# Decoder layer on one Trainium2 core: weighted sums of the attention moved directly behind the bursts of scores

## The chip, the cores and the metric

One core of a Trainium2 chip. The engines are PE (TensorE; PEld is its loading of weights), DVE (VectorE), ACT (ScalarE) and POOL (GpSimd); all DMAs are issued by SP (SyncE) on one queue. The metric is the device time of one execution in microseconds, as the median of several runs.

## The reference

For 32 batches of 128 positions with 1024 features in float32: attention with 32 query heads and 8 key and value heads, then a convolution with three taps weighted by cosine similarities of a context, then a low-rank mixture, each added to its input and normalised. The change touches the attention alone:

```python
q = (hidden_states @ wq.T).reshape(b, s, N_HEADS, HEAD_DIM).transpose(0, 2, 1, 3)
k = (hidden_states @ wk.T).reshape(b, s, N_KV_HEADS, HEAD_DIM).transpose(0, 2, 1, 3)
v = (hidden_states @ wv.T).reshape(b, s, N_KV_HEADS, HEAD_DIM).transpose(0, 2, 1, 3)
q = q * cos[None, None] + _rotate_half(q) * sin[None, None]
k = k * cos[None, None] + _rotate_half(k) * sin[None, None]
...
scores = jnp.einsum('bhqd,bhkd->bhqk', q, k) / math.sqrt(HEAD_DIM)
...
attn = jax.nn.softmax(final, axis=-1)
out = jnp.einsum('bhqk,bhkd->bhqd', attn, v)
```

With 128 positions every key that is not in the future is allowed, so the mask is the causal one.

## The kernel before

The program has two parts with a barrier between them. Part 1 (`part1`, from line 144) computes projections, scores, softmax and weighted sums for the 32 batches and stores the sums in `ot_scratch`; part 2 (`part2`, line 886) does the output projection, the convolution, the mixture and the norms. Part 2 starts on every engine only when all engines have ended part 1.

Part 1 is a software pipeline written out by hand: each engine has a function `step(t, par)` that `steps` (line 86) calls for t = 0 to 33, most of them in a hardware loop. In step t PE projects batch t (keys and values, then two groups of queries, in 24 slots of three 128x512 matmuls: `project`, line 433), and works on the scores of batch a = t - 1 and the weighted sums of batch b = t - 2. A batch has two halves u = 0, 1 of its heads. Ahead of the projection of certain slots PE does:

- slots 1 and 13: `score` (line 463), a burst of 16 matmuls with 32 rows each, placed side by side in the array; four banks `s_ps` take them. A profile counts each float32 matmul of this kind twice;
- slot 9: `turn_q` of half 1 (transposes of queries, line 452); slot 22: that of half 0 of the next batch; slot 17: `turn_k` (transposes of keys, line 442);
- slot 9, behind the transposes: `weigh` (line 476) of half 0, four matmuls with 32 columns each; slot 17, ahead of `turn_k`: `weigh` of half 1. Both write the one bank `pv_ps`.

Around it: DVE rotates the projections (`rotate`, lines 545 to 553; for the keys it also copies the new values into `v_new`), then for each of eight groups p = 0 to 7 adds the mask and takes the minimum (`mask_min`, 563), inverts the sums (570) and transposes 32x32 blocks (`turn_p`, 578). ACT rounds x (`high_x`, 668), squares the context (676), copies turned queries and keys (`copy_q` 682, `copy_k` 687) from the one bank `turn_ps`, takes the exponentials (695) and reads `pv_ps` (`read_ot`, 706: half 0 at p = 3, half 1 at p = 6). POOL scales the probabilities (814) and adds the rotated parts. SP's `step` (line 371) issues in this order: the loads of x and of the context, `move_p(b, 1)`, which is ten DMAs from `blocks` to `pt` (line 306), the store of half 0 of `ot`, the store of the sums `csum`, `move_v(t)` (line 296: `v_new` to `v_t`), `move_p(a, 0)`, and the store of half 1. SP works in order, so each wait in this list holds what is behind it.

In the last steps (t = 31 to 33) the weights of part 2 are loaded and rounded, the output of the first two batches is loaded back and projected by PE in step 32, and ACT takes the root of the norms (`take_root`, 727) at the end of step 32.

Of the kernel before, what the change touches and what calls it, by code (L numbers as in the profile page):

```python
# [22 lines left out]
B, S, D = 32, 128, 1024  # L23
# [35 lines left out]
def after(t, per, k):  # L59

    return t * per + k
# [7 lines left out]
def wait(eng, sem, count):  # L69

    if isinstance(count, int) and count <= 0:
        return
    eng.wait_ge(sem, count)


def valid(t):

    return not isinstance(t, int) or 0 <= t < B
# [65 lines left out]
def part1(nc, ctx, weights, raw, halves, wo_ps, handoff, xT, ctx_in, wqkv, wo, wx, wb,  # L144
# [135 lines left out]
    @block.sync  # L280
    def _(sp):
        def load_x(t, par):
            wait(sp, x_lo, after(t - 2, 2, 2))
            sp.dma_start(xraw[:, par], xT[t]).then_inc(x_in[par], 16)

        def load_ctx(t):
            wait(sp, sq_done, after(t - 1, 1, 1))
            wait(sp, nb_done, after(t - 1, 2, 2))
            first = ctx_in[t, 0, 0:1]
            sp.dma_start(ctx_t[:], bass.AP(tensor=first.tensor, offset=first.offset,  # L290
                                           ap=[[CB * S, P], [1, (CB + 1) * S]])).then_inc(c_in, 16)

        def move_v(t, par):
            wait(sp, pv_done, after(t - 2, NU, NU))
            wait(sp, rope_read, after(t, NG, 1))
            sp.dma_start(v_t[:, par], v_new[:]).then_inc(v_in, 16)

        def move_p(a, u):

            if at_step(a, 0):  # L300
                sp.wait_ge(set_up, 2)
            wait(sp, turned, after(a, NC, NJ * (u + 1)))
            wait(sp, pv_done, after(a - 1, NU, u + 1))
            for qb in range(QB):
                for kb in range(qb + 1):
                    sp.dma_start(pt[kb * SB:(kb + 1) * SB, u, qb], blocks[qb * SB:(qb + 1) * SB, u, kb]
                                 ).then_inc(p_in[u], 16)

        def load_later(n):

            if n == 0:
                wait(sp, x_lo, 2 * B)
            elif n == 1:
                wait(sp, sq_done, B)
                wait(sp, nb_done, 2 * B)
            elif n == 2:
                wait(sp, sq_done, B)
            else:
                later_done(sp, max(m for m in range(n) if lands(m) == lands(n)))
            dst, arrived = landing[lands(n)], later_in[lands(n)]  # L320
            if n < KT:
                sp.dma_start(dst, wo[:, n, :]).then_inc(arrived, 16)
            elif n == KT + 1:
                sp.dma_start(dst, wb).then_inc(arrived, 16)
            else:
                sp.dma_start(dst[:, 0:TAPS * P], wx).then_inc(arrived, 16)

        def load_o(t):

            wait(sp, x_lo, 2 * (B - 1 + t))  # L330
            if t == 1:
                later_done(sp, KT - 2)
            for u in range(NU):
                wait(sp, ot_out[u], after(t, 16, 16))
            sp.dma_start(raw[:, t], ot_dram[t]).then_inc(o_in[t], 16)

        def load_sums():

            sums = cs_dram[0, 0, 0:1]
            sp.wait_ge(cs_out, 16 * B)  # L340
            sp.wait_ge(summed, B)
            for dst, at, width in ((sqs, 0, QD + 1), (nbs, D, QD)):
                sp.dma_start(dst, bass.AP(tensor=sums.tensor, offset=sums.offset + at,
                                          ap=[[2 * D, B], [QD, 4], [1, width]])).then_inc(cs_in, 16)

        def store_zeros():

            sp.wait_ge(set_up, 1)
            for row in range(2):
                sp.dma_start(sim_dram[:, row, 0:1], zero[0:B, :],  # L350
                             allow_slow_non_contiguous=True).then_inc(sim_out, 16)

        def store_own():

            sp.wait_ge(sim_made, 1)
            sp.dma_start(sim_row(sim_dram, 2, 0), own).then_inc(sim_out, 16)

        sp.dma_start(xraw[:, 0], xT[0]).then_inc(x_in[0], 16)
        for n in range(PIECES):
            wait(sp, w_lo, n - STAGES + 1)  # L360
            sp.dma_start(stage(n), wqkv[n // GP, :, (n % GP) * WK:(n % GP + 1) * WK, :]).then_inc(w_in[n % STAGES], 16)
            if n == GP + 1:
                sp.dma_start(rope_t[:], rope).then_inc(consts_in, 16)
                sp.dma_start(mask_t[:], mask).then_inc(consts_in, 16)
                sp.dma_start(id_t[:], ident).then_inc(consts_in, 16)
        load_x(1, 1)
        load_ctx(0)
        load_x(2, 0)
        store_zeros()

        def step(t, par):
            a, b = t - 1, t - 2
            if valid(t + 1):
                if not at_step(t, 0) and not at_step(t, 1):
                    load_x(t + 1, 1 - par)
                load_ctx(t + 1)
            if at_step(t, B - 1):
                load_later(0)
                load_later(1)
                load_o(0)  # L380
            if at_step(t, B):
                load_sums()
                load_later(5)
                load_later(6)
            if valid(b):
                move_p(b, 1)
                wait(sp, ot_read, after(b, NU, 1))
                sp.dma_start(ot_dram[b, :, 0:BANK], ot[:, 0]).then_inc(ot_out[0], 16)
            if at_step(t, LAST):
                store_own()  # L390
            if at_step(t, B):
                load_later(7)
                load_later(8)
                load_o(1)
                wait(sp, q_turned, NU * B)
                sp.dma_start(xn0[:], x[0]).then_inc(xn_in[0], 16)
            if valid(t):
                wait(sp, sq_done, after(t, 1, 1))
                wait(sp, summed, after(t, 1, 1))
                sums = cs_dram[t, 0, 0:1]  # L400
                sp.dma_start(bass.AP(tensor=sums.tensor, offset=sums.offset, ap=[[CB, P], [D, 2], [1, CB]]),
                             csum[:]).then_inc(cs_out, 16)
                move_v(t, par)
            if at_step(t, B - 1):
                load_later(2)
            if valid(a):
                move_p(a, 0)
            if at_step(t, B - 1):
                load_later(3)
            if at_step(t, B):  # L410
                load_later(9)
            if valid(b) and not at_step(b, B - 1):
                wait(sp, ot_read, after(b, NU, 2))
                sp.dma_start(ot_dram[b, :, BANK:D], ot[:, 1]).then_inc(ot_out[1], 16)
            if at_step(t, B - 1):
                load_later(4)

        steps(sp, step, 0, LAST, LEAD, TAIL)
        sp.wait_ge(ot_out[0], 16 * B)
        sp.wait_ge(ot_out[1], 16 * (B - 1))  # L420

    @block.tensor
    def _(pe):
# [70 lines left out]
                mm.then_inc(wo_done, 1)  # L494

        def step(t, par):
            a, b = t - 1, t - 2
            if at_step(t, 0):
                for s in range(SLOTS):
                    if s == 2 * KT:  # L500
# [7 lines left out]
            for s in range(SLOTS):  # L508
                if valid(a):
                    if s % (NJ * PERIOD) == 1:  # L510
                        score(a, 1 - par, s // (NJ * PERIOD))
                    if s == 9:
                        turn_q(a, 1)
                if valid(b):
                    if s == 9:
                        weigh(b, par, 0)
                    if s == 17:
                        weigh(b, par, 1)
                if valid(t):
                    if s == 17:  # L520
                        turn_k(t)
                    if s == 22:
                        turn_q(t, 0)
                    if not (at_step(t, 1) and s < AHEAD):
                        project(t, par, s // KT, s % KT)
                if at_step(t, B) and s % PERIOD > 0:
                    project_out(s % PERIOD - 1, s // PERIOD)
# [136 lines left out]
    def _(act):  # L664
# [68 lines left out]
            nc.scalar.copy(halves[:, t, 0].rearrange("p t s -> p (t s)"), raw[:, t]).then_inc(o_hi, 1)  # L733

        def step(t, par):
            a, b = t - 1, t - 2
            if at_step(t, 0):
                copy_k(0, 0)
                high_x(1, 1)
# [5 lines left out]
            for p in range(NC):  # L745
                if p == 3 and valid(a):
                    copy_q(a, 1)
                if p == 2 and valid(t + 1):
                    high_x(t + 1, 1 - par)
                if p == 3 and valid(b):  # L750
                    read_ot(b, 0)
                if p == 6 and valid(b):
                    read_ot(b, 1)
                if p == 6 and valid(t):
                    copy_k(t, par)
                if p == 7 and valid(t):
# [20 lines left out]
                        high_later(9)  # L777
            if at_step(t, B):
                take_root()

        steps(act, step, 0, LAST, LEAD, TAIL)

# [703 lines left out]
```

## Time and profile before

| | |
|---|---|
| Runs | 1433.77 us median of 3 (1432.33 to 1434.33) |
| Profiled execution | 1433.92 us, its span 1432.1 us |
| PE busy | 1366.3 us (95%), mean granted clock 0.981 |
| DVE, ACT, POOL busy | 1091.3, 931.8, 985.1 us (76%, 65%, 69%) |
| Part 1 | to about 780 us |

The span runs from the first to the last instruction of the profile, and the execution's own time is 1.8 us longer. Busy shares are averages over two parts with different limits. Of a line in the timeline the start is exact for matmuls, and its length is modelled: matmuls that follow each other overlap.

### The profile page before, as it was taken

How to read it: one execution, taken by the hardware profiler on the slowest of the kernel's cores; microseconds unless marked ns; L12 is line 12 of the kernel's file. 1: busy time of each engine (PE TensorE's matmuls, PEld its weight loads, DVE VectorE, ACT ScalarE, POOL GpSimd, SP SyncE). 2: the span in 40 equal slices, each digit the busy share in tenths (PEclk: the TensorE clock that was granted, in tenths of full speed). 3: DMA queues.
4: the chain of work that ended last, by engine and by line, in shares of the span. 5: the costliest groups of instructions: out<-in, count | busy, mean ns of one | idle time of the engine just before them, and what ended most of it. 6: DMA issues, size and time to landing. Idle time of an engine off the chain costs nothing. (4 is left out here: it accounts for less than half of the span.)

```text
span 1432.1 us, 32297 instructions
## 1 busy us (share of the span) xinstructions
PE 1366.3 (95%) x8288; PEld 1058.1 (74%) x8288; DVE 1091.3 (76%) x3869; ACT 931.8 (65%) x3258; POOL 985.1 (69%) x936
## 2 busy tenths in 40 slices
PE   6899999999999999999986799999999999999995
PEld 4677777777777777777753688888888888888873
DVE  5677777777777777777775487788887788887774
ACT  5787878788787887878874354555554555554543
POOL 3776777777777777777764666777776777776763
PEclk9999999999999999999996999999999999999997
DMA  7345445454454544545465866665666665656641
GB/s 242 105 124 152 148 119 152 118 153 135 128 152 120 156 125 135 153 118 154 123 189 173 203 151 166 176 151 158 163 157 163 176 153 157 165 154 162 160 118 45
DMA packets 108861, 213.03 MB, mean 149 GB/s; under 512 B 26640, under 2 KB 32272, under 8 KB 108816
## 3 DMA queue, kind: packets, MB, share of 16 engines
q1 hardware_dynamic: 108816, 212.51, 53.6%
q8 instruction: 18, 0.29, 0.1%
q14 instruction: 27, 0.22, 0.1%
HBM read 131.83 MB, written 34.47 MB: 116 GB/s over the span
## 5 line engine op out<-in xcount | busy, mean ns | idle before, releaser
L433 PE MATMUL wo_ps<-weights,halves 128*128 128x512 f32 x2304 | 572.2, 400 | 11.5 <-DVE weights L612 11.4
L433 PEld LDWEIGHTS wo_ps<-weights,halves 128*128 128x128 f32 x2304 | 422.8, 189 | 128.3 <-issue 34.3
L695 ACT ACTIVATE pexp<-sm,smin 128x128 f32<-128x128 f32 x1024 | 398.8, 393 | 123.5 <-DVE smin L563 121.6
L1043 PE MATMUL wo_ps<-weights,halves 128*128 128x512 f32 x1488 | 400.5, 402 | 2.0 <-DVE yz L1146 2.0
L814 POOL TENSOR_TENSOR pn<-pexp,prec 128x512 f32<-128x512 f32 x256 | 268.5, 1049 | 146.5 <-DVE prec L570 146.5
L1396 POOL TENSOR_TENSOR prods<-prod,prods 128x512 fp32r<-128x512 f32 x192 | 259.7, 1360 | 134.3 <-ACT prods L1290 129.2
L1043 PEld LDWEIGHTS wo_ps<-weights,halves 128*128 128x128 f32 x1488 | 273.0, 190 | 60.8 <-issue 3.7
L563 DVE CUSTOM_DVE_ANT_0 sm<-s_ps,mask_t 128x128 f32<-128x128 f32 x1024 | 231.9, 281 | 79.2 <-PE s_ps L463 79.0
L1290 ACT CAST prods<-prod 128x512 fp32r<-128x512 f32 x192 | 118.8, 621 | 165.7 <-DVE prod L1180 129.2
L1180 DVE TENSOR_TENSOR prod<-att,x 128x512 f32<-128x512 f32 x192 | 186.2, 985 | 13.7 <-DMA att<-sim_scratch 10.8
L695 ACT ACTIVATION_READ_ACCUMULATOR pexp<-sm,smin 128x1 f32 x1024 | 195.0, 190 | 0.0
L1054 PE MATMUL conv_ps<-prods,weights 128*128 128x512 f32 x576 | 168.0, 401 | 14.4 <-POOL prods L1396 14.4
L578 DVE STREAM_TRANSPOSE blocks<-pn 128x512 f32<-128x512 f32 x256 | 177.2, 692 | 1.6 <-POOL pn L814 1.5
L1054 PEld LDWEIGHTS conv_ps<-prods,weights 128*128 128x128 f32 x576 | 108.6, 190 | 43.1 <-POOL prods L1396 18.6
L1390 POOL TENSOR_TENSOR rstd<-var,power 128x1 f32<-128x1 f32 x96 | 76.7, 799 | 70.5 <-DVE var L1171 69.2
L1163 DVE BATCH_NORM_STATS2 stats<-yz 128x6 f32<-128x512 f32 x128 | 88.9, 695 | 4.4
L1384 POOL TENSOR_TENSOR halves<-raw,halves 128x512 fp32r<-128x512 f32 x60 | 90.4, 1508 | 2.0 <-ACT halves L1285 2.0
L463 PEld LDWEIGHTS s_ps<-kt,qt 32*128 32x128 f32 x2048 | 63.7, 188 | 31.1 <-issue 23.1
L570 DVE RECIPROCAL prec<-psum_row 128x4 f32<-128x4 f32 x256 | 44.9, 175 | 53.5 <-ACT pexp L695 53.1
L788 POOL TENSOR_TENSOR halves<-raw,halves 128x512 fp32r<-128x512 f32 x62 | 79.6, 1284 | 8.4 <-ACT halves L668 7.9
L563 DVE DVE_READ_ACCUMULATOR2_ANT smin<- 128x1 f32 x1024 | 84.9, 83 | 0.0
L795 POOL TENSOR_TENSOR nb<-ctx_t 128x512 f32<-128x512 f32 x64 | 82.5, 1290 | 1.6 <-DVE csum L591 1.6
(99 smaller groups left out, 1657.0 us busy)
## 6 DMA issues: line engine op xcount, KB each, us to landing
att<-sim_scratch SPq DMA_DIRECT2D x192, 252.0 KB
pt<-blocks SPq DMA_DIRECT2D x640, 64.0 KB, 2.0
ctx_t<-in_ctx SPq DMA_DIRECT2D x32, 576.0 KB, 4.4
raw<-in_xT SPq DMA_DIRECT2D x32, 512.0 KB, 3.7
raw<-ot_scratch SPq DMA_DIRECT2D x32, 512.0 KB, 6.5
xn<-in_x SPq DMA_DIRECT2D x32, 512.0 KB, 7.3
out<-late SPq DMA_DIRECT2D x32, 512.0 KB, 6.2
ot_scratch<-ot SPq DMA_DIRECT2D x63, 256.0 KB, 2.1
```

Source lines behind the costliest of these rows:

```text
L433: mm = pe.matmul(qkv_ps[(par + g) % 2][:], xs[:, par, xl, k], w_sb[:, wl, g, k], start=(k == 0 and n == 0), stop=(k == KT - 1 and n == 2))
L563: ins = dve.tensor_tensor_reduce(sm[:, c % 2, i * P:(i + 1) * P], s_ps[i][:, j * P:(j + 1) * P], mask_t[:], 1.0, 3e38, ALU.add, ALU.min, s ...
L578: dve.transpose(blocks[:, u, :, j], pn[:, c % 2].rearrange("p (i b k) -> p b i k", i=NI, b=QB)).then_inc(turned, 1)
L695: ins = nc.scalar.activation(pexp[:, c % 2, i * P:(i + 1) * P], sm[:, c % 2, i * P:(i + 1) * P], ACT.Exp, bias=smin[:, c % 2, i:i + 1], sc ...
L814: pool.tensor_tensor(pn[:, c % 2].rearrange("p (i s) -> p i s", i=NI), pexp[:, c % 2].rearrange("p (i s) -> p i s", i=NI), prec[:, c % 2]. ...
L1043: mm = pe.matmul(wo_ps[n][:], os_t[:, par, ol, k], wo_sb[:, wl, k, n * BANK:(n + 1) * BANK], start=(k == 0 and m == 0), stop=(k == KT - 1 ...
L1054: mm = pe.matmul(conv_ps[h][:], wx_sb[:, wl, k], prods[:, m % PB, xl], start=(k == 0 and n == 0), stop=(k == TAPS - 1 and n == 2))
L1163: dve.bn_stats(stats[n][:, half], src[:, half * BANK:(half + 1) * BANK]).then_inc(counted[n], 1)
L1180: dve.tensor_tensor(prod[:, m % PB], att[:, k, h * BANK:(h + 1) * BANK], x1[:, par, h * BANK + k:h * BANK + k + BANK], ALU.mult).then_inc( ...
L1290: nc.scalar.copy(prods[:, m % PB, 0], prod[:, m % PB]).then_inc(prod_hi, 1)
L1384: pool.tensor_tensor(lo, oraw[:, par, cols], hi.bitcast(F32), ALU.subtract).then_inc(o_lo, 1)
L1396: pool.tensor_tensor(prods[:, m % PB, 1], prod[:, m % PB], prods[:, m % PB, 0].bitcast(F32), ALU.subtract).then_inc(prod_lo, 1)
```

## The change

- PE: `weigh` of half 0 moves from slot 9 (behind the transposes of queries) to slot 13, directly behind the second burst of scores. `weigh` of half 1 moves from slot 17 to slot 1 of the following step, directly behind the first burst. In the last step (t = 33) half 1 of the last batch stays in slot 17.
- ACT: `read_ot` of half 0 moves from p = 3 to p = 5, that of half 1 from p = 6 to p = 1 of the following step; for the last batch it stands at the end of step 33.
- SP: `move_v(a)` is issued a step later, between the loads and `move_p(b, 1)`; the wait for the first weighted sum stands ahead of the store of `csum` instead of in `move_p(a, 0)`; the store of half 1 stands behind `move_p(b, 1)` a step later, and that of half 0 at the end of the step. In the last step the store of half 1 of batch 30 stands ahead of `move_p(31, 1)`.

```diff
 (SP, move_p)
-            wait(sp, pv_done, after(a - 1, NU, u + 1))
+            if u == 1:
+                wait(sp, pv_done, after(a - 1, NU, NU))
...
 (SP, step)
-            a, b = t - 1, t - 2
+            a, b, c = t - 1, t - 2, t - 3
+            if at_step(t, 1):
+                move_v(0, 0)
...
-            if valid(b):
+            if valid(a) and not at_step(t, 1):
+                move_v(a, 1 - par)
+            if valid(b) and not at_step(t, LAST):
                 move_p(b, 1)
-                wait(sp, ot_read, after(b, NU, 1))
-                sp.dma_start(ot_dram[b, :, 0:BANK], ot[:, 0]).then_inc(ot_out[0], 16)
+            if valid(c):
+                wait(sp, ot_read, after(c, NU, 2))
+                sp.dma_start(ot_dram[c, :, BANK:D], ot[:, 1]).then_inc(ot_out[1], 16)
+            if at_step(t, LAST):
+                move_p(b, 1)
             if at_step(t, LAST):
                 store_own()
...
+            if valid(a):
+                wait(sp, pv_done, after(a - 1, NU, 1))
             if valid(t):
                 wait(sp, sq_done, after(t, 1, 1))
                 wait(sp, summed, after(t, 1, 1))
...
-                move_v(t, par)
...
-            if valid(b) and not at_step(b, B - 1):
-                wait(sp, ot_read, after(b, NU, 2))
-                sp.dma_start(ot_dram[b, :, BANK:D], ot[:, 1]).then_inc(ot_out[1], 16)
+            if valid(b):
+                wait(sp, ot_read, after(b, NU, 1))
+                sp.dma_start(ot_dram[b, :, 0:BANK], ot[:, 0]).then_inc(ot_out[0], 16)
...
 (PE, step)
-                if valid(b):
-                    if s == 9:
-                        weigh(b, par, 0)
-                    if s == 17:
-                        weigh(b, par, 1)
+                if s == 1 and valid(c):
+                    weigh(c, 1 - par, 1)
+                if s == 1 + NJ * PERIOD and valid(b):
+                    weigh(b, par, 0)
+                if s == 17 and at_step(t, LAST):
+                    weigh(b, par, 1)
...
 (ACT, step)
-                if p == 3 and valid(b):
+                if p == 1 and valid(c):
+                    read_ot(c, 1)
+                if p == 5 and valid(b):
                     read_ot(b, 0)
-                if p == 6 and valid(b):
-                    read_ot(b, 1)
...
             if at_step(t, B):
                 take_root()
+            if at_step(t, LAST):
+                read_ot(b, 1)
```

In PE's program a full step reads so before, from its first burst of scores (`s_ps`) over the transposes of queries (`turn_ps<-id_t,xn`), the weighted sums (`pv_ps`) and the transposes of keys (`id_t,kx`):

```order
L463 MATMUL s_ps<-kt,qt 128x128 x16
L433 MATMUL wo_ps<-weights,halves 128x512 x24
L452 MATMUL turn_ps<-id_t,xn 128x128 x4
L476 MATMUL pv_ps<-pt,v_t 32x512 x4
L433 MATMUL wo_ps<-weights,halves 128x512 x12
L463 MATMUL s_ps<-kt,qt 128x128 x16
L433 MATMUL wo_ps<-weights,halves 128x512 x12
L476 MATMUL pv_ps<-pt,v_t 32x512 x4
L442 MATMUL turn_ps<-id_t,kx 128x128 x2
```

and so with the change (lines are nine further down, 472 is `score`, 485 `weigh`):

```order
L472 MATMUL s_ps<-kt,qt 128x128 x16
L485 MATMUL pv_ps<-pt,v_t 32x512 x4
L442 MATMUL wo_ps<-weights,halves 128x512 x24
L461 MATMUL turn_ps<-id_t,xn 128x128 x4
L442 MATMUL wo_ps<-weights,halves 128x512 x12
L472 MATMUL s_ps<-kt,qt 128x128 x16
L485 MATMUL pv_ps<-pt,v_t 32x512 x4
L442 MATMUL wo_ps<-weights,halves 128x512 x12
L451 MATMUL turn_ps<-id_t,kx 128x128 x2
```

Both weighted sums now stand behind bursts, the 24 and the two times 12 projections are as many as before, and each kind of transpose has projections on both sides.

At the end of part 1 SP issues before, from the load of `wb` on (`[waits ...]` names the semaphores that an instruction waits for; `ot_read` counts ACT's reads of `pv_ps`):

```order
L324 DMA ctx_t<-in_wb 128x1024 [waits later_lo_dve]
L414 DMA ot_scratch<-ot 128x512 [waits ot_read]
L306 DMA pt<-blocks 32x512 [waits pv_done,turned]
L306 DMA pt<-blocks 32x512 x9
L388 DMA ot_scratch<-ot 128x512 [waits ot_read]
L356 DMA sim_scratch<-raw 32x4x256 [waits sim_made]
L137 UNCONDITIONAL_BRANCH [waits ot_out1,ot_out0]
```

and with the change:

```order
L325 DMA ctx_t<-in_wb 128x1024 [waits later_lo_dve]
L423 DMA ot_scratch<-ot 128x512 [waits ot_read]
L394 DMA ot_scratch<-ot 128x512 [waits ot_read]
L307 DMA pt<-blocks 32x512 [waits pv_done,turned]
L307 DMA pt<-blocks 32x512 x9
L357 DMA sim_scratch<-raw 32x4x256 [waits sim_made]
L423 DMA ot_scratch<-ot 128x512 [waits ot_read]
L137 UNCONDITIONAL_BRANCH [waits ot_out1,ot_out0]
```

Ahead of the last ten moves now stand two stores. The second, L394, is that of half 1 of batch 30, which in the program before stood in step 32 as L414; it waits for a read that ACT does in step 33, behind `take_root`.

## Rows read from the trace of the kernel before

**Rows 1.** Busy time in a stretch: PE, PEld, DVE, ACT, POOL; clock, DMA share, GB/s.
```profile
82.50:712.60 630.10, 630.10 (x4537) 463.63 (x4536) 491.94 (x2465) 510.44 (x2409) 460.25 (x421) 1.00 0.46 138
```
**Rows 2.** Timeline of PE, part of a step: start, length, line, what, [idle before].
```profile
404.27 0.60 PE L452 MATMUL turn_ps<-id_t,xn 128*128 128x128 f32 x4
404.80 1.07 PE L476 MATMUL pv_ps<-pt,v_t 128*32 128x512 f32 x8
405.80 3.01 PE L433 MATMUL wo_ps<-weights,halves 128*128 128x512 f32 x12
408.74 0.98 PEld L463 LDWEIGHTS s_ps<-kt,qt 32*128 32x128 f32 x32 [0.35 <-issue]
408.74 1.17 PE L463 MATMUL s_ps<-kt,qt 32*128 32x128 f32 x32
409.85 3.01 PE L433 MATMUL wo_ps<-weights,halves 128*128 128x512 f32 x12
412.79 1.06 PE L476 MATMUL pv_ps<-pt,v_t 128*32 128x512 f32 x8
413.79 0.44 PE L442 MATMUL turn_ps<-id_t,kx 128*128 128x128 f32 x2
413.98 3.66 PE L433 MATMUL wo_ps<-weights,halves 128*128 128x512 f32 x15
417.48 0.60 PE L452 MATMUL turn_ps<-id_t,qn 128*128 128x128 f32 x4
417.84 2.33 PE L433 MATMUL wo_ps<-weights,halves 128*128 128x512 f32 x9
420.10 1.17 PE L463 MATMUL s_ps<-kt,qt 32*128 32x128 f32 x32
```
**Rows 3.** Timeline of DVE and ACT behind the second burst of that step.
```profile
412.22 0.69 DVE L545 TENSOR_TENSOR rot<-wo_ps,rope_t 128x512 f32<-128x512 f32 x1 [0.43 <-PE wo_ps L433]
...
415.94 0.56 ACT L706 COPY ot<-pv_ps 128x512 f32<-128x512 f32 x1
416.40 0.36 ACT L687 COPY kt<-turn_ps 128x256 f32<-128x256 f32 x1
```
**Rows 4.** Timeline of SP and ACT; last, the page's issues (KB, us to landing).
```profile
399.63 0.36 SPq L284 DMA_DIRECT2D raw<-in_xT  x1
...
402.68 6.21 SPq L306 DMA_DIRECT2D pt<-blocks  x10
...
415.06 6.21 SPq L306 DMA_DIRECT2D pt<-blocks  x10
...
404.39 1.05 ACT L668 CAST halves<-raw 128x1024 fp32r<-128x1024 f32 x1 [1.00 <-DMA raw<-in_xT]
...
406.89 0.56 ACT L682 COPY qt<-turn_ps 128x512 f32<-128x512 f32 x1
...
raw<-in_xT SPq DMA_DIRECT2D x32, 512.0 KB, 3.7
```
**Rows 5.** Timeline of SP and PE, steps 1 and 2.
```profile
56.50 1.45 SPq L296 DMA_DIRECT2D v_t<-v_new  x1
...
71.22 1.17 PE L463 MATMUL s_ps<-kt,qt 32*128 32x128 f32 x32 [1.36 <-ACT qt L682]
```
**Rows 6.** Timeline of PE, second burst of step 31.
```profile
724.68 1.17 PE L463 MATMUL s_ps<-kt,qt 32*128 32x128 f32 x32 [0.82 <-ACT qt L682]
```
**Rows 7.** Timeline of PE, SP and ACT at the end of part 1.
```profile
752.24 2.09 PE L463 MATMUL s_ps<-kt,qt 32*128 32x128 f32 x32 [3.00 <-ACT qt L682]
...
768.80 6.21 SPq L306 DMA_DIRECT2D pt<-blocks  x10
...
772.39 0.57 ACT L706 COPY ot<-pv_ps 128x512 f32<-128x512 f32 x1
...
776.45 1.94 PE L476 MATMUL pv_ps<-pt,v_t 128*32 128x512 f32 x8 [7.61 <-DMA pt<-blocks]
...
780.36 1.19 PE L1043 MATMUL wo_ps<-weights,halves 128*128 128x512 f32 x2 [1.97 <-DVE yz L1146]
```

More of the change, by code:

```diff
@@ L496, in step @@
         def step(t, par):
-            a, b = t - 1, t - 2
+            a, b, c = t - 1, t - 2, t - 3
             if at_step(t, 0):
@@ L735, in step @@
         def step(t, par):
-            a, b = t - 1, t - 2
+            a, b, c = t - 1, t - 2, t - 3
             if at_step(t, 0):
```

## The prediction

> **What bounds the kernel now.** I read the busy time by stretches first [rows 1]. Over 630.1 us, 28 steps of the attention half at 22.50 each, PE is busy for all 630.1 at the full granted clock, while DVE has 491.9, ACT 510.4 and POOL 460.3. PE sets the pace there, and what can be won is what PE spends when it goes from one shape of tile to another. The timeline of PE from one transpose of queries to the next first burst [rows 2] shows that. Starts are what counts in it; the length of a block overlaps with what follows. The reader is to see:
> - Twelve projections and the change to a weighted sum take 412.79 - 409.85 = 2.94, nine and the change to scores 420.10 - 417.84 = 2.26: three fewer for 0.68, 0.227 for one.
> - Fifteen before a transpose take 417.48 - 413.98 = 3.50; less three, 2.82. So leaving full-size matmuls for tiles of 32 costs 0.12 more than leaving them for a transpose.
> - Transpose to weighted sum takes 404.80 - 404.27 = 0.53, transpose to projection 417.84 - 417.48 = 0.36: 0.17 less.
> - Score burst to projection takes 409.85 - 408.74 = 1.11, weighted sum to projection 405.80 - 404.80 = 1.00, weighted sum to transpose 413.79 - 412.79 = 1.00. What a weighted sum costs does not depend on which of the two follows.
>
> **The change, part by part.** Durations are from the profiled execution, 1433.92 us around a span of 1432.1. That is 0.15 over the median of the three runs; the difference is put on the median, 1433.77. A measurement of this kernel can tell about 0.2%, 2.9 us, from no change.
>
> *PE, a full step.* The first weighted sum no longer follows a transpose, so that transpose goes into projections: -0.17. The second no longer ends twelve projections; they end in the transpose of the keys: -0.12. That transpose now stands behind a full matmul; 413.98 - 413.79 = 0.19 is what it takes behind a weighted sum, two transposes of the queries' kind take 0.36 / 2 = 0.18 or, less a change, under that, so I bound the gain by 0 and 0.05 and take 0.03. The change from scores to a weighted sum stands in no row. The nearest row leaves a burst at 1.11 for projections; I take that and no extra, and the rivals have the other end. Sum: -0.32 a step, to 22.18. Steps 3 to 30 are 28: -9.0.
>
> *What the weighted sums delay.* Both bursts now have 1.00 of weighted sum behind them, so the projection behind each ends 1.00 later against its burst. DVE's rotation at 412.22 waits for just that projection [rows 3]; so it, the masks behind it and the exponentials behind those move by 1.00. ACT's copy of the turned keys ends at 416.76. The read ahead of it, 415.94 to 416.40, is gone (-0.46), so it ends 0.54 later against the burst. PE's transpose at 417.48 needs it: 0.72 of slack, less 0.54, less the 0.15 that PE gains in this half, leaves 0.03. That is a tie, and hundredths may go.
> The ten moves of probabilities on SP start at 415.06 behind DVE, and now 1.00 later; the load of x stands behind them [rows 4]. Against the next first burst, itself 0.1 nearer, it is 1.1 later. From its issue at 399.63 to ACT's rounding at 404.39 it takes 4.8 here, and ACT waited 1.00 for it; the copy of the queries ends at 407.45, 1.29 before the second burst at 408.74. Less 1.1, and less the 0.2 that PE gains before that burst, nothing is left. But this is a slow load: the page's median is 3.7, which leaves about 1 us. For both ties together I give back 0.4 over the loop, so it is worth -8.6.
> Covered, at nothing: ACT's read of the previous second sum (about 0.57), now ahead of the second exponential, lies in the wait for x; without that cover it would move the copy of the queries by 0.57. SP's move of the new values (put at one move's 0.62) now stands between the loads and the ten moves at 402.68. These start 3.05 behind the load of x with one other load between, so over 2 us are free, and the values are needed by a rotation that starts only with the last projections before 404.27; without the cover the ten moves, and so nothing before the weighted sum 20 us later, would wait. SP now waits for the first weighted sum, over 2.1 behind the second burst, before it stores the sums of squares; the ten moves behind start 415.06 - 408.74 = 6.3 behind the burst, so the wait ends first.
>
> *Start.* In step 2 the second burst waits at 71.22, 1.36 of it idle, for a copy that is behind x [rows 5]. The move of the values at 56.50, 1.45 long, stands ahead of ten moves and that load. It goes behind the load, so the burst comes 1.45 earlier; PE is ready for it, as the weighted sum no longer stands ahead of it. With the second half of that step: -1.6.
>
> *Step 31.* The load of the first attention output is again issued behind the ten moves, so 1.1 later, and the second burst at 724.68 waits for what follows from it, 0.82 already [rows 6]. What comes after hangs on this burst: +1.1. A load of weights no longer stands behind SP's wait for the second weighted sum and may free some of what follows; the bounds are 0 and -1.1 (it cannot give more than the delay), and I take 0, since no row shows that it held anything.
>
> *The end of the attention half* [rows 7]. The last ten moves are issued at 768.80 and land for the weighted sum at 776.45; part 2 begins on PE at 780.36, behind it and a barrier. The changed SP first stores the second sum of batch 30, which ACT must have read, and ACT reads it only behind the square root, in the place where it reads the first sum of batch 31 now: 772.39. ACT has one read more ahead of the second burst at 752.24, which waits for ACT: +0.57, so 772.96, and the read ends at 773.5. Then 0.1, a store of 0.62, ten moves of 6.21, and the 1.44 from the moves' end (775.01) to the sum: 781.9 against 776.45, +5.4. Part 2 can start nothing before, so this is paid in full.
>
> **Sum:** -1.6 - 8.6 + 1.1 + 5.4 = -3.7, so **1430.1 us**. Over half of what the loop gains is given back at the end.
>
> A rule beside the trace: in the rows PE pays when it enters or leaves tiles of 32. The Trainium skill (TensorEngine Tiling (Array Packing), Key Properties) says that "Changing tiling mode (not just tile) drains the TensorE". By it the change from the row tiles of the scores to the column tiles of the weighted sum is one more drain, so a step goes from eight changes of mode to six; it gives no price. With the rows' 0.12 to 0.17 as the price of one, two fewer would be worth 0.24 to 0.34 a step, where my differences give 0.32.
>
> **Rivals.**
> *A, slower: scores to weighted sum is a dear change.* No row has it. The first weight load of a burst stands idle for 0.35 before 408.74 [rows 2]. If the column tiles wait that long for the row tiles on top of the 1.11, twice a step, the step gains 0.32 and loses 0.70: 28 x 0.38 = +10.6, with -1.6 + 1.1 + 5.4 = +4.9: 1449. With an extra of 0.12 each, as for leaving full matmuls, 0.08 a step is left: -2.2 + 4.9 makes 1436.5. It decides from 0.10 a change on, where the loop's 28 x 0.12 = 3.4 no longer pays for the 4.9. Against it: the weighted sum's own leaving is the same for two followers. Chance 0.13, half for each price.
> *B, the later load of x becomes the bound.* If it takes 4.8 and a little more in all steps, the second burst waits some 0.2 in each: 28 x 0.12 = -3.4 in place of -8.6, so 1435.3. For it: ACT waits for x in the step shown. Against: the median of 3.7. Chance 0.12.
> *C, the end costs nothing*, as something else holds part 2: -9.1, 1424.7. Against it: the 7.61 that PE stands idle for these very moves. Chance 0.08.
>
> **How the numbers follow.** The forecast has 0.67, and by itself lies between 1427.5 and 1432.5: the loop -7.0 (0.25 a step) to -9.9 (0.35), step 31 up to 1.1 lower, the end 4.5 to 6. The range is 1425.5 to 1435.5, which takes in B and part of C and leaves A out. Faster by over 0.2% means below 1430.9: C and 0.75 of the forecast, 0.58. Slower means above 1436.6: the dear half of A and some of the other half, 0.10. The rest, 0.32, lies within.
>
> **What would show it.** In the profile after: steps of 22.2 with PE busy throughout; the weighted sum 1.1 behind the start of a burst and 1.0 to the projections; hundredths of idle time for the copies of keys and queries; x rounded about 1 us later behind the first burst; the second burst of step 2 near 69.7; the last ten moves behind a read that follows the square root, the last two weighted sums both behind it and some 8 us apart, and part 2's first matmul near 776.6 (780.36 - 3.7). Steps above 22.3 would make the loop's term wrong, over 1.2 from burst to weighted sum would be A, a second burst that waits in each step B, and a first matmul of part 2 near 771 C.

## The result, and the profile after

The changed kernel takes **1447.84 us** (median of 4 runs, 1445.97 to 1451.50) against 1433.05 for the kernel before on the same chip (4 runs, 1431.35 to 1434.33): ratio 1.011, 95% interval 1.0091 to 1.0128. It is slower, by 15 us, where 3.7 faster was forecast. The profiled execution has a span of 1444.1 against 1432.1, so 12.0 us are there to be found. (This execution is 1.9 below the median of its kernel and the one before 0.9 above its own, which makes the rest.)

The busy time of PE in the 28 full steps, with the same columns as [rows 1], comes first:

```profile
85.50:717.20 631.70, 624.37 (x4537) 462.55 (x4536) 488.94 (x2465) 512.59 (x2410) 460.45 (x421) 1.00 0.47 137
```

PE's work in this stretch fell from 630.10 to 624.37, 0.20 a step: the changes between shapes of tile are cheaper, as forecast. But the stretch got longer, 631.7. PE now stands idle for 7.3 us in it, and did not before. The waits of the whole execution (engine, line, what it waited for: us in total, times, longest) name the cause:

```profile
DVE v_new L563 <- DMA v_t<-v_new: 50.3, 31, 4.4
...
PE s_ps L472 <- DVE smin L573: 15.9, 18, 4.3
```

Before, DVE's copy into `v_new` waited for the move of the values once, 0.7 us. Now it waits in every step but the first. One such step, SP, DVE and PE, in the timeline (start, length, line, what, [idle before]):

```profile
225.72 0.36 SPq L284 DMA_DIRECT2D raw<-in_xT  x1
226.34 0.35 SPq L290 DMA_DIRECT2D ctx_t<-in_ctx  x1
226.91 0.52 SPq L296 DMA_DIRECT2D v_t<-v_new  x1
```
```profile
230.55 0.41 DVE L560 TENSOR_TENSOR rot<-wo_ps,rope_t 128x256 f32<-128x256 f32 x1
233.46 0.42 DVE L563 COPY v_new<-wo_ps 128x256 f32<-128x256 f32 x1 [2.50 <-DMA v_t<-v_new]
```
```profile
234.78 1.17 PE L472 MATMUL s_ps<-kt,qt 32*128 32x128 f32 x32 [1.10 <-DVE smin L573]
```

The reader is to see one chain. `v_new` is a single buffer. The move out of it is issued at 226.91, right behind 1.1 MB of loads, and has not landed when the next values are ready at 230.96. DVE waits 2.50 with the minima of the next masks (`smin`) queued behind the copy, and the second burst needs the banks that these masks free: PE waits 1.10. It does so in 15 of the 28 steps. The row on how long the move takes from issue to landing, of the kernel before and of the changed one:

```profile
DMA to landing us min/median/max: 2.0/2.0/3.0
```
```profile
DMA to landing us min/median/max: 2.1/5.2/7.3
```

A step that this wait does not reach looks as forecast (ten of the 28 lie within 0.01 of it):

```profile
627.49 1.17 PE L472 MATMUL s_ps<-kt,qt 32*128 32x128 f32 x32
628.59 1.06 PE L485 MATMUL pv_ps<-pt,v_t 128*32 128x512 f32 x8
629.59 5.75 PE L442 MATMUL wo_ps<-weights,halves 128*128 128x512 f32 x24
635.18 0.60 PE L461 MATMUL turn_ps<-id_t,xn 128*128 128x128 f32 x4
635.54 3.02 PE L442 MATMUL wo_ps<-weights,halves 128*128 128x512 f32 x12
638.48 1.17 PE L472 MATMUL s_ps<-kt,qt 32*128 32x128 f32 x32
639.59 1.07 PE L485 MATMUL pv_ps<-pt,v_t 128*32 128x512 f32 x8
640.58 3.04 PE L442 MATMUL wo_ps<-weights,halves 128*128 128x512 f32 x12
643.45 0.38 PE L451 MATMUL turn_ps<-id_t,kx 128*128 128x128 f32 x2
643.59 3.70 PE L442 MATMUL wo_ps<-weights,halves 128*128 128x512 f32 x15
647.12 0.63 PE L461 MATMUL turn_ps<-id_t,qn 128*128 128x128 f32 x4
647.50 2.32 PE L442 MATMUL wo_ps<-weights,halves 128*128 128x512 f32 x9
649.75 1.17 PE L472 MATMUL s_ps<-kt,qt 32*128 32x128 f32 x32
```

It takes 649.75 - 627.49 = 22.26, where 22.18 was forecast. Burst to weighted sum is 1.10, weighted sum to projections 1.00. Rival A's dear change does not exist.

Step 2, which answers to [rows 5], and step 31, to [rows 6], on PE:

```profile
72.08 2.09 PE L472 MATMUL s_ps<-kt,qt 32*128 32x128 f32 x32 [4.32 <-DVE smin L573]
74.10 1.94 PE L485 MATMUL pv_ps<-pt,v_t 128*32 128x512 f32 x8
...
731.20 1.38 PE L472 MATMUL s_ps<-kt,qt 32*128 32x128 f32 x32 [2.93 <-DVE smin L573]
732.51 1.94 PE L485 MATMUL pv_ps<-pt,v_t 128*32 128x512 f32 x8
```

Both second bursts wait for the same masks. Behind the longer idle time the burst and the weighted sum of step 2 take 2.09 and 1.94 in place of 1.17 and 1.06: they run at 1.2 GHz, not 2.4. In step 31 they take 1.38 and 1.94, and the granted clock is 0.66 over 731 to 736. The windows around step 2 (the number before the last two is the granted clock) say so:

```profile
57.00:70.00 13.00, 10.62 (x75) 8.19 (x73) 7.69 (x40) 10.23 (x52) 10.13 (x9) 0.99 0.58 167
70.00:76.00 6.00, 3.92 (x41) 2.06 (x41) 4.67 (x22) 2.85 (x14) 3.45 (x4) 0.50 0.28 70
```

The end of part 1, which answers to [rows 7], on ACT, SP and PE:

```profile
777.50 1.04 ACT L725 CAST weights<-ctx_t 128x1024 fp32r<-128x1024 f32 x1 [3.84 <-DMA ctx_t<-in_wb]
...
780.18 0.57 ACT L716 COPY ot<-pv_ps 128x512 f32<-128x512 f32 x1
```
```profile
780.77 0.34 SPq L394 DMA_DIRECT2D ot_scratch<-ot  x1
781.21 6.22 SPq L307 DMA_DIRECT2D pt<-blocks  x10
```
```profile
780.89 1.93 PE L485 MATMUL pv_ps<-pt,v_t 128*32 128x512 f32 x8 [9.28 <-ACT ot L716]
788.87 1.94 PE L485 MATMUL pv_ps<-pt,v_t 128*32 128x512 f32 x8 [6.04 <-DMA pt<-blocks]
792.78 2.47 PE L1055 MATMUL wo_ps<-weights,halves 128*128 128x512 f32 x5 [1.98 <-DVE yz L1158]
```

This is the mechanism of the forecast: the read behind the square root, the store, the ten moves, and two weighted sums 8.0 apart.

The 12.0 us, cut at the starts of PE's first bursts of steps 2, 3, 31 and 32 and at part 2's first matmul, beside the experiments below (the stretches are from single profiled executions, in us; the last column but one is the ratio to the kernel before that was run beside each, and the last the median of its own runs; the kernel before had 1433.05 beside the changed kernel and 1431.75 to 1431.93 beside e1 to e10):

| kernel | step 2 | steps 3 to 30 | step 31 | step 32 to part 2 | ratio (95%) | median |
|---|---|---|---|---|---|---|
| before | 24.87 | 630.09 | 24.17 | 43.55 | | |
| changed | 27.76 | 631.73 | 27.09 | 48.48 | 1.0110 (1.0091 to 1.0128) | 1447.84 |
| e1 | 25.11 | 624.69 | 24.63 | 50.06 | 1.0016 (1.0004 to 1.0028) | 1434.71 |
| e2 | 25.95 | 624.98 | 24.82 | 48.60 | 1.0021 (1.0008 to 1.0033) | 1434.57 |
| e3 | 28.40 | 632.59 | 27.36 | 44.34 | 1.0077 (1.0060 to 1.0094) | 1444.39 |
| e4 | 27.76 | 632.49 | 24.59 | 42.99 | 1.0031 (1.0018 to 1.0044) | 1437.61 |
| e5 | 23.62 | 626.31 | 26.27 | 44.57 | 0.9988 (0.9979 to 0.9997) | 1429.71 |
| e6 | 27.33 | 627.95 | 29.12 | 42.48 | 1.0016 (1.0002 to 1.0031) | 1433.94 |
| e7 | 24.78 | 621.97 | 27.18 | 44.48 | 0.9958 (0.9945 to 0.9972) | 1426.40 |
| e8 | 25.18 | 623.58 | 27.18 | 50.40 | 1.0026 (1.0016 to 1.0036) | 1435.92 |
| e9 | 23.09 | 621.97 | 22.39 | 45.61 | 0.9932 (0.9916 to 0.9948) | 1422.56 |
| e10 | 24.53 | 630.09 | 23.29 | 43.67 | 0.9994 (0.9983 to 1.0004) | 1431.67 |

So +2.9, +1.6, +2.9 and +4.9 for the change; what lies ahead and part 2 make up the rest (-0.4).

### The profile page after: what moved, and what is told of

It reads as the page before. It is cut to its first block and busy times, and to the rows that moved or that the text cites. A ratio compares the mean times of both kernels' runs of the same rounds, so it can differ in the third digit from the quotient of the medians.

```text
span 1444.1 us, 32306 instructions
## 1 busy us (share of the span) xinstructions
PE 1362.7 (94%) x8288; PEld 1057.7 (73%) x8288; DVE 1089.8 (75%) x3869; ACT 934.6 (65%) x3258; POOL 983.4 (68%) x936
## 5 line engine op out<-in xcount | busy, mean ns | idle before, releaser
L472 PE MATMUL s_ps<-kt,qt 32*128 32x128 f32 x2048 | 77.1, 288 | 21.8 <-DVE smin L573 15.9
L821 POOL TENSOR_TENSOR qn<-rot 128x512 f32<-128x512 f32 x32 | 41.4, 1293 | 71.7 <-DVE rot L560 71.7
```

What stands on the lines that cost most here:

```text
L472: mm = pe.matmul(s_ps[i][:, j * P:(j + 1) * P], qt[rows, u, j * P:(j + 1) * P], kt[rows, par, u * P:(u + 1) * P], start=True, stop=True, t ...
```

## The experiments

The theory, called V: the single buffer `v_new`, held by a move that lands late behind the loads, costs the loop its gain and disturbs steps 2 and 31. Its rivals stand in each expectation by their letters (X is the later load of x, D a DVE that has become too full). For the end there is theory E: the store ahead of the last moves costs about 4.

**e1: a second buffer for the new values.**

```diff
-    v_new = sb("v_new", [P, KV])
+    v_new = sb("v_new", [P, 2, KV])
...
-            sp.dma_start(v_t[:, par], v_new[:]).then_inc(v_in, 16)
+            sp.dma_start(v_t[:, par], v_new[:, par]).then_inc(v_in, 16)
...
-                wait(dve, v_in, after(t, 16, 0))
-                ins = dve.tensor_copy(v_new[:], src[:, KV:2 * KV])
+                wait(dve, v_in, after(t - 1, 16, 0))
+                ins = dve.tensor_copy(v_new[:, par], src[:, KV:2 * KV])
```

> The changed kernel with two buffers for the new values, so that the copy into v_new no longer waits for the move of the batch before. Theory V (the late move of the values holds DVE, and through the masks the second burst): no wait of DVE for v_t<-v_new, all full steps at the 22.27 us that the undisturbed ones have now (28 x 0.29 = 8 us less), the start of step 2 about 4 us less, step 31 about 2 us less; 1433 to 1435 us. Theory X (the late load of x holds the second burst): steps stay at 22.5 to 22.6 and PE waits for ACT's copy of the queries; 1443 to 1447 us. Theory D (DVE as a whole has become too full, the wait for the values only fills a gap): likewise above 1442 us, with PE waiting for the masks.

The move still lands late, but DVE is gone from those who wait, and POOL, whose work follows the copy, waits at the two ends alone, as it did before:

```profile
who waited for it (us, times):
  POOL kx L814: 15.4, 2
...
DMA to landing us min/median/max: 2.4/5.3/7.1
```

The loop falls by 7.0 against the changed kernel, to 22.31 a step, and the time from 1.0110 to 1.0016 of the kernel before. V holds: the wait, not the transfer, was the cost. The rivals X and D fall, since the load of x and the work of DVE are as they were. At the end e1 gives 1.6 back. Of this, 0.9 lies ahead of the second burst of step 32, which waits for ACT's copy (16.45 behind the first burst, 15.52 in the changed kernel), and 0.7 in the last ten moves, which SP issues in 6.93 here and in 6.22 there; what lies behind either was not tried.

**e2: the same move, issued ahead of the two loads.**

```diff
+            if valid(a) and not at_step(t, 1):
+                move_v(a, 1 - par)
             if valid(t + 1):
...
-            if valid(a) and not at_step(t, 1):
-                move_v(a, 1 - par)
             if valid(b) and not at_step(t, LAST):
```

> The changed kernel with one buffer, but the move of the values issued ahead of the loads of x and of the context. Theory V with the queue as its cause (the 0.13 MB wait behind the 1.1 MB of both loads): landing back from 5.2 to about 2 to 2.5 us, no wait of DVE for the values, while x comes 0.6 us later and takes some of it back: steps of 22.3 to 22.45 us, 1435 to 1440 us. If the landing is late for another reason (the write itself, the wait for the weighted sum), it stays near 5 us and the time near 1447 us.

```profile
  DVE v_new L563: 0.5, 1
...
DMA to landing us min/median/max: 2.0/2.1/4.9
```

The single buffer is back, and the wait is gone all the same: with the loads behind it the move lands in 2.1, not 5.2. So it is the place behind the loads that makes it late. The time, 1434.57, is just below the range.

**e4: the kernel before, with the move of the values alone a step later**, in the place that the change gives it (between the loads and `move_p(b, 1)`).

```diff
+            if at_step(t, 1):
+                move_v(0, 0)
...
+            if valid(a) and not at_step(t, 1):
+                move_v(a, 1 - par)
             if valid(b):
                 move_p(b, 1)
...
-                move_v(t, par)
```

> The kernel before with nothing changed but the move of the values, issued a step later behind the loads of x and the context, as in the changed kernel. Theory V: landing near 5 us here too, DVE waits for it over 1 us a step, but in this order the projection of the keys ends 1 us earlier against the burst and the second burst is 0.2 us later, so that little of it reaches PE: 1433 to 1438 us. If the late move alone were the whole loss, 1446 us or more; if the landing is 2 us here, the queue is not what made it late.

```profile
DVE v_new L556 <- DMA v_t<-v_new: 49.2, 31, 3.9
```

The wait is as long as in the changed kernel, 49.2 against 50.3, with nothing else of the change in it, and the time is inside the range. Step 2 takes 27.76 as in the changed kernel. But the loop lost only 2.4. In the kernel before, DVE's copy into `v_new` starts 3.95 ahead of the second burst (median of steps 3 to 30); with the change and no wait, in e1, it starts 2.69 ahead, because the first weighted sum no longer stands between the keys' projection and that burst (e6, which moves that sum alone, has 2.78). Where the wait holds the burst, the copy starts 1.32 ahead of it. So the old order takes up 2.6 of waiting before PE feels it, and the new one 1.4. The median wait is 1.3 in e4 and 1.6 in the changed kernel: most waits fit into the old order's room, and 15 of 28 do not fit into the new one's. The part is worth +0.3% alone and 0.9% in the whole: costs of this kind do not add.

**e8: the changed kernel, with x loaded one load earlier**, so that only the context stands ahead of the move. The loop's load goes from the start of the step, `load_x(t + 1, 1 - par)`, to a place ahead of `move_p(a, 0)` in the step before, as `load_x(t + 2, par)`.

> The changed kernel with the load of x alone moved ahead of the ten moves one step earlier, so that only the load of the context (0.58 MB) is in front of the move of the values, not x (0.52 MB) as well. If the landing is late by what is queued ahead of it, it falls from 5.2 us to 3 to 4 us, DVE waits less than 0.8 us a step, PE's waits for the masks go in most steps: 1438 to 1442 us. If the landing does not fall, the loads ahead are not its cause, and the time stays at 1445 us or more.

```profile
DVE v_new L563 <- DMA v_t<-v_new: 7.7, 6, 4.4
...
DMA to landing us min/median/max: 2.7/3.8/7.5
```

It went further than expected, 1435.92 against 1438 to 1442. The move lands in 3.8 in the median (not 5.2), which is below the 4 that the copy leaves it. In step 31, where three half-megabyte loads stand ahead of the move, DVE still waits 4.45, and the step takes 27.18. Three ways to make the move early enough, or not needed, give the same time within 0.1%.

**e3: the last ten moves ahead of the store.** In the last step `move_p(b, 1)` stands where it stands in all others, ahead of the store of half 1 of batch 30.

> The changed kernel with, in step 33 alone, the last ten moves ahead of the store of the second sum of batch 30. Theory E (the end is late since these moves stand behind that store): the ten moves start near 775.8 instead of 781.2 in the time of the changed kernel, part 2 starts 5 us earlier, 1442 to 1443.5 us. If part 2 is held by something else (the read of the sums behind the square root), under 2 us are won, 1446 us or more.

```profile
783.62 1.94 PE L483 MATMUL pv_ps<-pt,v_t 128*32 128x512 f32 x8 [9.69 <-ACT ot L714]
786.34 1.94 PE L483 MATMUL pv_ps<-pt,v_t 128*32 128x512 f32 x8 [0.79 <-ACT ot L714]
791.12 9.17 PE L1053 MATMUL wo_ps<-weights,halves 128*128 128x512 f32 x31 [2.84 <-DVE yz L1156]
```

The two sums are 2.7 apart, not 8.0, and the stretch to part 2 falls from 48.48 to 44.34. The ten moves now start at 778.35, ahead of the read at 782.91. E is right about the stretch. The time, 1444.39, is between the two ranges given: steps 2 to 31 of this execution happen to take 1.8 more than in the changed kernel, and the two ratios, 1.0077 and 1.0110, have intervals that overlap by 0.0003. The gain in the whole time is clear only between e1 and e5. What is left is the read behind the square root; ahead of the root ACT waits 3.98 for the load of `wb` (3.84 in the changed kernel).

**e5: e1 and e3 together.**

> The changed kernel with both single repairs together: two buffers for the new values, and the last ten moves ahead of the store of the second sum of batch 30. If the late values and the late end are two separate costs, this lies 4 to 5 us below the two buffers alone: 1429 to 1431 us, where before has about 1432, with full steps of 22.3 us and 43.5 to 45 us from the first burst of step 32 to part 2. If the end only waits for the next thing (the root, the sums of the cosine), it stays above 1433 us.

1429.71, ratio 0.9988: inside, and 0.28% below e1. With its two costs repaired, the change is barely worth having.

**e6: the first weighted sum alone.** The kernel before, with three edits; the second half, and the move of the values, stay where they were.

```diff
-                    if s == 9:
+                    if s == 1 + NJ * PERIOD:
                         weigh(b, par, 0)
...
-                if p == 3 and valid(b):
+                if p == 5 and valid(b):
                     read_ot(b, 0)
```

And SP stores half 0 behind the move of the values, no longer behind `move_p(b, 1)`.

> The kernel before with the first weighted sum alone moved behind the second burst (read at p = 5, its store behind the move of the values); second half and values where they were. By the price of its change of tiles this is worth 0.17 us a step, 22.33 us, so 4.8 us in the loop, less about 1 us in step 31, and nothing is lost at the end: 1428 to 1429.5 us, a ratio of 0.997 to 0.998. If the later projection of the second group of queries costs PE a wait, steps stay at 22.4 to 22.5 us and the time at 1431 to 1433 us.

A miss: 1433.94, ratio 1.0016, above both ranges. Full steps take 22.34, 0.16 less, just as the 0.17 for the transpose that now goes into projections says. But two of them, 4 and 5, take 23.45 and 23.44: x is rounded 5.6 and 4.7 behind its issue there, and the second burst stands idle 1.0 for the copy that follows. So the loop gains 2.1 and not 4.5. And steps 2 and 31 lose 2.5 and 4.9 in the profiled execution (itself 2.7 above the median of its runs):

```profile
70.26 1.58 PE L464 MATMUL s_ps<-kt,qt 32*128 32x128 f32 x32 [3.36 <-ACT qt L683]
71.78 1.94 PE L477 MATMUL pv_ps<-pt,v_t 128*32 128x512 f32 x8
...
726.25 2.09 PE L464 MATMUL s_ps<-kt,qt 32*128 32x128 f32 x32 [4.07 <-ACT qt L683]
728.27 1.72 PE L477 MATMUL pv_ps<-pt,v_t 128*32 128x512 f32 x8
```

The weighted sum that stood ahead of this burst filled 1.2 us of a wait for x (in step 31, for the first output). In step 2 of the kernel before it also cut PE's idle time in two, 0.90 ahead of it and 1.36 ahead of the burst:

```profile
65.85 1.06 PE L476 MATMUL pv_ps<-pt,v_t 128*32 128x512 f32 x8 [0.90 <-DMA pt<-blocks]
```

Where a load holds the burst, taking work from ahead of it gains nothing and puts 1.0 behind it; the idle time grows, and with it comes the lower clock: 1.52 and 1.86 for burst and sum in step 2, 2.02 and 1.64 in step 31, in place of 1.1 and 1.0. For step 2 that is the whole 2.5: -0.1 ahead of the burst, 1.0 for the sum, 1.6 for the clock. In step 31 the output's load also took 8.4 from issue to rounding (716.23 to 724.66), 6.3 before (716.79 to 723.09). Three loads are issued one behind the other there, the output's last, over 1.05 in e6 (from 715.18) and over 2.27 before (from 714.52); by my estimate that is 1.2 of the 2.1, and the rest stays open. No value waits for its move in this kernel, so this is a cost of the moved sum itself.

**e7: everything repaired.** e5, x early as in e8, and the copy of the keys one group earlier (`copy_k` at p = 5, ahead of the exponentials it followed).

> Both repairs, and two more: the load of x goes ahead of the ten moves of the first half one step earlier, and the copy of the turned keys on ACT ahead of the exponentials of p = 5. If the 0.1 us that a step of 22.27 us has over my sum of 22.18 is the tie at the keys and the late x, steps fall to 22.15 to 22.2 us, step 2 no longer waits for x, and the time is 1422 to 1427 us. If the sum itself was 0.1 us too low, steps stay at 22.27 us and only the start gains, 1427 to 1430 us.

1426.40, inside the range. All 28 full steps are 22.21, with PE busy throughout. In e8, with x as early and the copy of the keys where it was, 25 of them are 22.27. So the tie at that copy is worth 0.06 a step; e7 differs from e8 in the buffers too, but e1, which has them, also shows 22.27. In step 2 ACT no longer waits for x, as expected, but the second burst still stands idle 1.94 for ACT's copy.

**e9: e7, with the first output loaded ahead of the later weights in step 31.** Step 31 had become the dearest place: a half-megabyte load stands third of three.

```diff
             if at_step(t, B - 1):
+                load_o(0)
                 load_later(0)
                 load_later(1)
-                load_o(0)
```

> The kernel of e7 with one thing more: in step 31 SP loads the first attention output ahead of the two loads of later weights, not behind them. In e7's trace that load is issued at 708.33, third of three loads of half a megabyte within 1.1 us, and the second burst of that step waits 3.23 us idle, after which the burst takes 2.09 and the weighted sum behind it 1.72 instead of 1.17 and 1.06. Theory Q (the load waits its turn on the queue, and the idle time costs the clock on top): the output lands some 3 us earlier, the burst waits under 1.5 us and runs at full clock, step 31 falls from 27.18 by 3 to 4 us; what it gains partly returns at the burst of step 32, which waits 4.21. Time 1423 to 1426. Rival R (its own transfer is the limit, wherever it stands): step 31 stays near 27 and the time near e7's, 1426 to 1427.

```profile
709.87 1.05 ACT L741 CAST halves<-raw 128x1024 fp32r<-128x1024 f32 x1 [0.31 <-DMA raw<-ot_scratch]
...
712.19 1.17 PE L470 MATMUL s_ps<-kt,qt 32*128 32x128 f32 x32
```

Issued at 705.67, the output is rounded at 709.87, 4.2 behind; in e7 it was issued at 708.33 and rounded at 715.54, 7.2 behind. Step 31 falls from 27.18 to 22.39, and the burst and the sum behind it run at full clock again. 1422.56, ratio 0.9932: slightly below the range, and faster than both kernels. It is faster than e7 too, though the intervals of the two ratios overlap by 0.0003; step 31 in the traces makes the case. (In the traces step 2 is also 1.7 shorter than in e7, which the exchange cannot have done; the last section comes back to it.)

**e10: the kernel before, with that exchange alone.**

> The kernel before with the same exchange of loads in step 31 alone. There the second burst of that step waits only 0.82, so there is little to win. Theory Q: step 31 falls from 24.17 by about 0.8, some of it given back in step 32: 1430.5 to 1432 against 1431.8 for the kernel before. Rival R: no change, 1431 to 1432.5. If it wins more than 1.5 us, step 31 was holding more than its burst.

1431.67, ratio 0.9994: no difference that can be told. Step 31 gains 0.88, as expected, and no more. The same repair is worth five times as much in the new order. There the burst stands idle 3.23, not 0.82, as the weighted sum no longer fills the wait and the output is rounded 7.2 behind its issue, not 6.3; and the lower clock behind it costs 1.6, where before the burst ran at full clock.

## Why the prediction was wrong, point by point

**The step that failed** is the one put as "Covered, at nothing" for SP's move of the new values. I counted what it costs SP to issue (0.62) and found over 2 us free; I looked for who reads the values, and not for who writes `v_new` next. DVE's copy is ready 4.0 behind the issue (230.96 - 226.91), and the move needed 2.0 to land in its old place. Behind the two loads it needs 5.2. No row of mine had its landing. The Trainium skill (DMA: Bandwidth & Descriptors, Queues, rings and completion order) says that descriptors are consumed in ring order on each DMA engine, and that the semaphore's increment "lands only after every earlier write from that SDMA engine". By it a small move behind 1.1 MB waits for them, and e2 agrees: 2.1 in front of them, 5.2 behind. Whether the small move waits for its turn or shares the DMA engines with the loads, no run here separates. The rule was in reach of the prediction and was not used. The step is worth 7.0 in the loop, 2.7 in step 2 and 2.5 in step 31 (e1 against the changed kernel), 0.94% by the ratios.

**The loop** was forecast at -8.6, and is +1.6; without the wait (e1) it is -5.4, and with both ties loosened (e7) -8.1. The terms of PE: the sum -0.32 stands at -0.29 there (22.50 - 22.21). Burst to weighted sum 1.11 assumed, 1.10 found. The transpose into projections, 0.36 forecast, 0.36 found (635.54 - 635.18). Twelve projections into a transpose 2.82 forecast, 2.87 found. The transpose of the keys gained 0.05 (0.14 against 0.19), the upper bound. Fifteen projections took 3.53 or 3.54, up to 0.04 over. The tie at the keys' copy (0.03 of slack) was called, and its 0.4 for both ties was too little: the keys' 0.06 a step is 1.7 over the loop, and x, at 22.31 - 22.27 in e1, 1.1 more.

**Step 2** was forecast at -1.6 and is +2.9. The earlier load did what was said: without the wait for the values (e1) the second burst comes 12.21 behind the first, not 13.54, 1.33 of the 1.45. What I missed stands behind it: 2.13 of idle time ahead of that burst, where 1.36 had been, and the clock at half. Burst and sum then take 1.6 more, which left e1 at +0.2. (In e1 PE waits there for the copy of the queries, not for the values.)

**Step 31** was forecast at +1.1. In e1 the burst comes 0.94 later, as said; the rest in the changed kernel, another 1.0 of wait for the values and the slow clock, was in no term.

**The end** was forecast at +5.4 and costs 4.9. The size is right and e3 shows the mechanism: it takes 4.1 of it back in this stretch, and 5.5 beside the two buffers (e5 against e1). ACT's further read ahead of the second burst of step 32 was put at 0.57; that burst comes 0.1 later in the changed kernel, 0.3 in e3 and 1.0 in e1.

**The rivals.** A is refuted: 1.10, not 1.23 or more. Its dear half named 1449, close to the measured time, and that is chance. B is real but small: ACT rounds x 7.3 behind the first burst in e1, 6.0 before (medians), so 1.3 later where 1.1 was said, and the burst waits 0.48 and 0.35 for ACT's copy in two steps (e1's loop is 0.04 a step above its floor). The sign given for B, a second burst that waits, did appear in the changed kernel, but PE waited for DVE's masks and not for x. C is refuted by e3. What came true, a second wait in DVE, was not on the list. The account of e6 went wrong at another place: it asked what the moved sum costs, and not what it had been filling.

## What to carry to other kernels

Before a DMA is moved on a queue, look up its time from issue to landing and everything that waits for its landing, above all the next writer of its source; then ask what will stand ahead of it. Work that stands ahead of a burst which itself waits for a load costs nothing there, and taking it away gains nothing in those places; count the steps in which PE is the bound apart from the first and the last. An edit's worth depends on its neighbours: e4 alone +0.3%, in the whole 0.9%; the exchange of loads nothing before, 0.26% behind the repairs (e9's 0.9932 against e7's 0.9958).

## What the runs showed that I had not expected

A move of 128x256 values lands 2.0 us behind its issue with nothing large ahead (kernel before, median), 3.8 behind one load of 576 KB (e8), and 5.2 behind two, of 1088 KB together (changed kernel).

A wait of about 2 us ahead of a burst may or may not cost the clock. The programs of e7 and e9 differ in step 31 alone. Here is the second burst of step 2 in the one and in the other:

```profile
68.09 1.69 PE L470 MATMUL s_ps<-kt,qt 32*128 32x128 f32 x32 [1.94 <-ACT qt L690]
69.71 1.94 PE L483 MATMUL pv_ps<-pt,v_t 128*32 128x512 f32 x8
```
```profile
68.00 1.17 PE L470 MATMUL s_ps<-kt,qt 32*128 32x128 f32 x32 [1.80 <-ACT qt L690]
69.11 1.07 PE L483 MATMUL pv_ps<-pt,v_t 128*32 128x512 f32 x8
```

The granted clock over 68 to 72 is 0.57 in e7 and 1.00 in e9, and step 2 takes 24.78 against 23.09. The idle time alone does not decide it: in step 31 of e1 the burst was idle 1.93 and ran at full clock, and that of e5 was idle 2.02 and ran at half (the step takes 26.27 against 24.63); in step 2 of the two it is the other way round, e5's burst, 2.20 idle, at full clock and e1's, 2.13 idle, at half. What does decide stays open. So each such place is uncertain by about 1.6 us between executions, which is as much as some of the differences between single traces above. It may be a part of the spread between runs of one kernel; that was not tried by itself.
